# Running sums by head taken from a transposition of the running sums by token

## The reference, cut to what matters

```python
xn = _layernorm(x)
x_branch, z_branch = split(xn @ in_proj_w.T)
x_branch = silu(conv4(x_branch) + conv_b)
proj = x_branch @ x_proj_w.T            # X (1024), dt (16 heads), B (128), C (128)
dt = softplus(dt @ dt_proj_w.T + dt_proj_b)
A_scaled = -exp(A_log) * dt             # one number for each token and head
A_cumsum = cumsum(A_scaled)             # within a chunk
L = exp(A_cumsum[l] - A_cumsum[s])      # for s <= l, for each head
Y_diag = einsum(C, B, L, X * dt)
...                                     # the state of the chunks before, decayed
Y = (Y + X * D) * silu(z_branch)
x + Y @ out_proj_w.T + W3 (sigmoid(W1 xn) * (W2 xn))
```

## Time and profile before

| | |
|---|---|
| time, median of 3 runs | 1618.42 us (1616.63 to 1618.63) |
| the profiled execution, its own time | 1617.01 us |
| its span | 1615.2 us |
| busy: PE, DVE, ACT, POOL | 1559.1, 1203.7, 886.9, 495.6 us |
| mean granted clock of TensorE | 0.989 |
| block 0, from the start to the first sums (L571) | 65.0 us |
| distance of two later blocks, L571 to L571 (484.93 to 678.50) | 193.6 us |

### The profile page before, as it was taken

The page is one execution under the profiler, slowest core; times in us unless marked ns, Lnnn a source line. Parts: engine busy times, 40 slices in busy tenths (PEclk is TensorE's granted clock), DMA queues, the critical chain, the costliest instruction groups (busy, mean ns, idle before and its releaser), DMA issues.

```text
span 1615.2 us, 25318 instructions
## 1 busy us (share of the span) xinstructions
PE 1559.1 (97%) x9086; PEld 744.3 (46%) x9086; DVE 1203.7 (75%) x1876; ACT 886.9 (55%) x1840; POOL 495.6 (31%) x480
## 2 busy tenths in 40 slices
PE   7779899999999999999999999999999999999999
PEld 3334444544444444444444444444444544444444
DVE  7878776699566985689856897568966699576862
ACT  6687435565356644466454663646636565356641
POOL 3116664233033321234221431314303233033210
PEclk9799999999999999999999999999999999999999
DMA  7155430242402432133321333213350242402320
GB/s 266 55 168 175 140 105 14 62 104 74 89 27 68 99 97 56 37 86 85 85 53 47 81 97 92 26 60 89 84 103 14 66 106 71 87 27 73 97 67 26
DMA packets 228605, 131.66 MB, mean 82 GB/s; under 512 B 175200, under 2 KB 176992, under 8 KB 228480
## 3 DMA queue, kind: packets, MB, share of 16 engines
q1 hardware_dynamic: 228480, 130.05, 30.0%
HBM read 100.38 MB, written 29.62 MB: 80 GB/s over the span
## 4 chain that ended last, share of the span: by engine, by line
PE 62%; DVE 18%; issue 7%; ACT 5%; DMA 2%; POOL 2%; SPq 1%; DVEq 0%; POOLq 0%; ACTq 0%
PE bank L723 12%; PE bank L613 11%; PE bank L741 9%; PE bank L507 9%; PE bank L523 6%; PE bank L533 4%; DVE edc L1365 4%; PE bank L696 4%; DVE xst_lo L1336 2%; ACT edc L985 2%; PE bank L645 1%; DVE xin L1407 1%; DVE xdt L1315 1%; ACT mdc L997 1%; DVE xs L1414 1%
## 5 line engine op out<-in xcount | busy, mean ns | idle before, releaser
L613 PE MATMUL bank<-wx_hi,arena 128*128 128x512 f16 x1024 | 319.7, 382 | 0.0
L723 PE MATMUL bank<-xt_hi,q 128*128 128x512 f16 x704 | 267.0, 379 | 4.0 <-issue 4.0
L723 PE MATMUL bank<-xt_lo,q 128*128 128x512 f16 x704 | 267.0, 379 | 0.0
L1688 POOL TENSOR_TENSOR xst<-xdt,dst 128x512 f32<-128x512 f32 x60 | 62.6, 1043 | 490.3 <-DVE xdt L1315 490.3
L613 PE MATMUL bank<-wx_lo,arena 128*128 128x512 f16 x512 | 195.9, 383 | 0.0
L741 PE MATMUL bank<-q,arena 128*128 128x512 fp8e4 x704 | 163.3, 381 | 0.0
L985 ACT ACTIVATE edc<-csl,csv 128x128 f32<-128x128 f32 x512 | 155.8, 389 | 0.8 <-DMA csl<-sums 0.8
L1365 DVE TENSOR_TENSOR edc<-edc,gt 128x512 f32<-128x512 f32 x128 | 125.9, 1022 | 38.7 <-ACT edc L990 38.6
L613 PEld LDWEIGHTS bank<-wx_hi,arena 128*128 128x128 f16 x1024 | 101.1, 99 | 114.7 <-issue 3.7
L1024 ACT CAST arena<-full 128x512 f16<-128x512 f32 x88 | 54.2, 616 | 146.4 <-DVE full L1444 146.4
L1709 POOL TENSOR_TENSOR xin<-xin,xs 128x512 f32<-128x512 f32 x60 | 83.8, 1397 | 153.0 <-DVE xin L1388 153.0
(11 more groups left out here) (217 smaller groups left out, 3419.2 us busy)
## 6 DMA issues: line engine op xcount, KB each, us to landing
csl<-sums SPq DMA_DIRECT2D x128, 256.0 KB, 3.6
y_squares<-xs SPq DMA_DIRECT2D x56, 256.0 KB, 2.0
xin<-y_squares SPq DMA_DIRECT2D x168, 64.0 KB, 2.5
xin<-x SPq DMA_DIRECT2D x32, 256.0 KB, 4.0
res<-x SPq DMA_DIRECT2D x32, 256.0 KB, 3.4
out<-res SPq DMA_DIRECT2D x32, 256.0 KB, 2.0
raw<-w_ffn SPq DMA_DIRECT2D x25, 256.0 KB, 2.9
x_squares<-mdc SPq DMA_DIRECT2D x24, 256.0 KB, 2.0
```

Of the source, the lines that this page charges most:

```text
L613: i = pe.matmul(banks[0][:], act[:, k, c * P:(c + 1) * P], wt[:, k, hf * half:(hf + 1) * half], start=(n == 1), stop=(n == 3 * ki))
L723: i = pe.matmul(up_bank(m, j)[:], q12[:, j, m, k, :], part[:, k, :], start=(n == 1), stop=(n == 2 * kd))
```

## The change

The four products L571 are gone. The sums by head now come from the sums by token: `csv`, 128 tokens by 64 columns (chunk and head), is turned by one transposition on PE (`turn_sums`) to 64 rows by 128 tokens. That instruction stands inside C's product, between its third and fourth part of eight, so behind 9 of 24 matmuls; in block 0, where C is done earlier, it stands behind the transposition of B. `csv` must therefore be there before: DVE's copy waits for the products alone, no longer for ACT. ACT's two exponentials wait for that copy, and ACT's copy to `cst` comes behind them, ahead of the high part of C. `cst` is 64 rows of 128 in place of 16 rows of 512, with the same 64 pieces of 512 bytes in DRAM.

```diff
-        cst = sb("cst", [heads, tb])
+        cst = sb("cst", [chunks * heads, P])
...
-                sp.dma_start(sums.rearrange("c h l -> h c l"),
-                             cst[:].rearrange("h (c l) -> h c l", c=chunks)).then_inc(D["sums_out"], DMA)
+                sp.dma_start(sums.rearrange("c h l -> (c h) l"), cst[:]).then_inc(D["sums_out"], DMA)
...
-            def project(b, bk, col):
+            def project(b, bk, col, between=lambda: None):
                 n = 0
                 for k in range(ki):
+                    if k == 3:
+                        between()
...
-                pe.wait_ge(S["acc"], at(b, "acc", 6))
-                for c in range(chunks):
-                    i = pe.matmul(banks[6][0:heads, c * P:(c + 1) * P], sml["av"][:, c, :], upp[:],
-                                  start=True, stop=True)
-                i.then_inc(S["cst_mm"], 1)
                 pe.matmul(banks[5][:, 0:w], upp[:], v["av"], start=True, stop=True)
                 pe.matmul(banks[5][:, w:2 * w], ones[:], v["av"], start=True, stop=True).then_inc(
                     S["cs_mm"], 1)
+
+            def turn_sums(b):
+                pe.wait_ge(S["acc"], at(b, "acc", 6))
+                pe.wait_ge(S["cs_rest"], at(b, "cs_rest", 0))
+                pe.transpose(banks[6][0:chunks * heads, 0:P], v["csv"], idn[:]).then_inc(S["cst_mm"], 1)
...
-                    project(b, c_bank(b), di + ns).then_inc(S["c_mm"], 1)
+                    project(b, c_bank(b), di + ns, lambda: turn_sums(b)).then_inc(S["c_mm"], 1)
                 turn_b(b)
+                if b == 0:
+                    turn_sums(b)
                 project_x(b, 0, lambda: gram(b))
...
+                act.wait_ge(S["cs_rest"], at(b, "cs_rest", 0))
+                act.activation(v["ecs"], banks[5][:, 0:w], ACT.Exp).then_inc(S["ecs_dec"], 1)
+                act.activation(v["dec"], banks[5][:, w:2 * w], ACT.Exp).then_inc(S["ecs_dec"], 1)
                 act.wait_ge(S["cst_mm"], at(b, "cst_mm", 0))
                 if b:
                     act.wait_ge(D["sums_out"], b * DMA)
-                act.copy(cst[:], banks[6][0:heads, :]).then_inc(S["cst"], 1)
-                act.wait_ge(S["cs_mm"], at(b, "cs_mm", 0))
-                act.activation(v["ecs"], banks[5][:, 0:w], ACT.Exp).then_inc(S["ecs_dec"], 1)
-                act.activation(v["dec"], banks[5][:, w:2 * w], ACT.Exp).then_inc(S["ecs_dec"], 1)
+                act.copy(cst[:], banks[6][0:w, 0:P]).then_inc(S["cst"], 1)
                 act.wait_ge(S["c_mm"], at(b, "c_mm", 0))
...
-                dve.wait_ge(S["ecs_dec"], at(b, "ecs_dec", 1))
+                dve.wait_ge(S["cs_mm"], at(b, "cs_mm", 0))
                 dve.tensor_copy(v["csv"], banks[5][:, 0:w]).then_inc(S["cs_rest"], 1)
                 dve.wait_ge(S["cs_rest"], at(b, "cs_rest", 0))
+                dve.wait_ge(S["ecs_dec"], at(b, "ecs_dec", 1))
```

## The result

The changed kernel takes 1619.72 us (median of 20 runs, 1616.49 to 1624.0), the kernel before 1617.43 beside it (20 runs, 1614.74 to 1620.3). That lies within the 0.2% that the forecast calls no difference, and within its range. But I had forecast 0.2 us less, and twenty runs of each tell the two apart: the sign is wrong, and the sum is 3 us off.

What follows compares the result with a forecast made beforehand. PE's work laid end to end was taken to bound the later blocks, ACT's copy of X to pace block 0. Seven later blocks -2.4 us and block 0 +2.2 gave -0.2 against 1618.4: 1618.2 us, range 1614.2 to 1621.8.

Steps and rivals of the forecast that it cites:

- PE's three terms: Later blocks, PE: C's product 0.92 us earlier, transposition adding 0.13, no standing for `csv`; net gain 0.79 a block.
- The wait of ACT for `csl`: Later blocks: ACT, drawn earlier by PE, waits 0.45 us for `csl` before its decay, a wait not there before.
- the +2.2 for X's copy: Block 0: ACT's copy of X, taken to set the pace, comes 2.2 us later, carried through the block.
- the case I took it from: Block 0: the clock rises as long after X's start as now, so X is done 2.05 us later.
- the case in which ACT's decay sets the copy: Block 0: the clock rises at the same time as now; the decay holds ACT to 80.6, +1.95 us.
- clock stays low: Block 0: PE runs X at 1.2 GHz to its end, costing 5.3 us; 1621.3 us in all; chance 0.05.
- the sum of the later blocks: Blocks 1 to 7: the scan starts 0.34 us earlier, all behind it shifted alike; -2.4 us in seven.
- I take 1.6: Later blocks: the sums' store, now from 64 partitions, lands 1.6 us after issue, 0.3 to either side.
- Slack enough: Later blocks: the sums are back before ACT asks, each block gains 0.79 us; 1615.1 us; chance 0.18.
- Block 0 absorbs its delay: Block 0: its delay vanishes in PE's idle time, leaving -2.4 us, 1616.0 us; chance 0.15.
- `csv` comes too late: Later blocks: `csv` over 1 us late, PE stands inside C; adds to the slower side; chance 0.03.
- The store takes longer: slower: Later blocks: store from 64 partitions, or transposition, takes longer; at 0.6 us more +4.0, 1622.4 us; chance 0.12.

Runs made afterwards that it cites:

- run 8: Kernel before, but storing a tile of zeros, 64 partitions by 128 columns, in place of the sums: 1618.23 us, ratio 1.0009.
- block0_only: Block 0 as in the changed kernel, blocks 1 to 7 as in the kernel before: 1619.92 us, ratio 1.0019.
- part2: Changed kernel with the transposition behind 6 of C's 24 matmuls in place of 9: 1616.70 us, ratio 0.9999.
- part6: Changed kernel with the transposition behind 18 of C's 24 matmuls in place of 9: 1636.64 us, ratio 1.0117.
- c_high_first: Changed kernel, but in block 0 ACT makes C's high part ahead of the exponentials and the copy to `cst`: 1619.70 us, ratio 1.0021.
- run 6: Changed kernel with block 0 as before; in later blocks transposition behind 3 matmuls, `csv` copied ahead of B's low part: 1612.38 us, ratio 0.9981.
- run 2: The same run as `block0_only`: kernel before with only block 0 as in the changed kernel: 1619.92 us, ratio 1.0019.
- runs 1 and 10: Changed kernel with block 0 as before the change; the same kernel timed twice: 1616.85 us, ratio 0.9995, then 1615.90 us, ratio 0.9988.
- run 4: The same run as `part6`: changed kernel with the transposition behind 18 of C's matmuls in place of 9: 1636.64 us, ratio 1.0117.
- runs 7 and 11: Changed kernel, `csv` copied before B's low part, in block 0 between weight splits and transposed before B; later transposition behind 3 matmuls: 1613.54 us; behind nine: 1616.75.

## Why the prediction was wrong

**The mechanisms held.** PE's three terms: C starts 0.47 us behind the first product (0.53 said), the transposition holds PE 0.11 (0.13), no stand for `csv`. ACT's copy takes 0.26 (0.28). The wait of ACT for `csl`, said to be 0.45, came in all seven blocks at 0.29 to 0.97, and the scan waits for `xdt_lo` in all seven. In block 0 the +2.2 for X's copy came as +2.18, though not by the case I took it from, X held back by a late clock. Stretches of the changed kernel, then of the kernel before (PEclk is the third number from the end):

```profile
74.00:76.00 2.00, 2.00 (x5) 0.68 (x6) 2.00 (x4) 0.24 (x2) 0.00 (x0) 0.50 0.18 38
76.00:78.00 2.00, 2.00 (x17) 1.41 (x16) 2.00 (x4) 0.04 (x1) 0.00 (x0) 0.70 0.81 231
```

```profile
74.00:76.00 2.00, 2.00 (x9) 0.80 (x7) 1.90 (x4) 1.79 (x5) 0.00 (x0) 0.69 0.37 121
```

The granted clock leaves its lower level 2.0 us later than before. Those are the 1.97 of this execution's late start: it came back at the same point of the block, and not 1.85 later with X. So the case in which ACT's decay sets the copy held, and X took less time. It is over well before ACT asks for it:

```profile
81.18 0.38 PE L614 MATMUL bank<-wx_hi,arena 128*128 128x512 f16 x1
```

X ends at 81.56 and is copied at 82.82, and the copy's row has no wait: ACT's 4.86 us from the decay's start set it. With my own figure for the decay that case gives +1.95; the decay came 0.23 later than I had it. The rival *clock stays low* falls with the same two rows.

**The step that failed is the sum of the later blocks**, "Behind that the block is as before, shifted by 0.34. Seven blocks: -2.4 us". Against before (16.38 us from the first product to the scan) the seven shifts are -0.21, -0.12, -0.34, -0.45, -0.47, +0.08 and +0.21: **-1.3 us** in all. By time, the two runs with the later blocks alone say -0.8 (-2.3 to +0.6) and -1.9 (-3.4 to -0.3), too wide to show the missing microsecond by themselves; it stands on the rows. The sizes in it, against my own working:

- *The store*, "I take 1.6". It took 1.8 in blocks 1 to 5; run 8 shows that its form does that. 0.2 in five blocks: +1.0 us. It was inside the bounds I gave (0.3), on the bad side.
- *The store in blocks 6 and 7*: 2.31 (1269.72 - 1267.41) and 2.26, so 0.7 over mine: +1.4. Nothing in my sum had it. The decay is there later than it was before the change. These are the stores of the section on the hardware below.
- *Up to the store's issue*: 3.00 us behind the first product (493.89 - 490.89), where my numbers give 3.11: -0.8 in seven.
- *The first load*, from its issue to ACT's start: 3.45 in block 2, 3.09 in block 5 (1079.38 - 1076.29), where I had 3.33 in all. In the seven together -0.7.

They come to +0.9, and the scan's shift is off by +1.1; 0.13 of the rest is block 3, where the second half of `csl` took 3.99 us to land and the relus that need it came later. Rows of SP and ACT in block 6 of the changed kernel:

```profile
1267.41 0.48 SPq L385 DMA_DIRECT2D sums<-cst  x1
1269.72 13.90 SPq L397 DMA_DIRECT2D csl<-sums  x6
```

```profile
1272.87 2.44 ACT L988 ACTIVATE edc<-csl,csv 128x128 f32<-128x128 f32 x8 [0.84 <-DMA csl<-sums]
```

**Block 0's term was taken from one profile.** Its +2.2 is inside the interval of the +3.1 (1.5 to 4.5) timed. But among six profiles with block 0 as before, that one has X's copy latest: 13.68 us behind the first product of the sums, where the others have 12.69 to 13.46, and all six 13.05 on average. The four with block 0 as in the change (`block0_only`, `part2`, `part6` and the changed kernel) have 15.77, so +2.7. From the first products of block 0 to those of block 1 the six have 227.2 us on average (225.8 to 228.2), the four 229.5 (228.6 to 230.0): +2.3. The changed kernel's own profile against that of before has +4.05, one nearly the shortest of its kind, the other the longest; taking that for the term would be reading noise. PE's granted clock fell twice for 6.8 us between 184 and 204 us there, where before has one fall of 3.4 us. The stretch of the second fall, changed kernel, then before:

```profile
190.00:200.00 10.00, 6.83 (x30) 3.03 (x28) 7.45 (x12) 1.12 (x2) 6.68 (x5) 0.67 0.04 6
```

```profile
190.00:200.00 10.00, 6.71 (x34) 3.34 (x35) 6.03 (x12) 2.93 (x6) 5.43 (x4) 1.00 0.47 156
```

All four profiles with the change's block 0 have these two falls of 6.8 us; the six others have falls of 3.4 to 10.2 us in all in this stretch. No experiment shows whether the later X brings them about.

**The sum.** The halves timed alone give +3.1 and, from both runs, -1.4: +1.7, against +2.9 (1.8 to 4.0) for the whole. I had +2.2 and -2.4. The later blocks gave a microsecond less than I had it, and that has its rows, above. Block 0 cost 0.9 more by time and 0.1 to 0.5 more by the profiles, and the whole cost 1.2 more than its halves; both are within what these medians tell, and neither is assigned.

One place where more can go is behind the scan. "Behind that the block is as before" didn't hold in the changed kernel's profile: up to the scan its blocks 1 to 6 gained 1.5 us, but from block 1's first product to block 7's it takes 1161.6 us, as before (1160.2 to 1161.7 in four profiles). PE's wait for `xt_lo` took 1.9 us there against 0.5. By the chain of work it ends with another load from DRAM, `xin<-x_squares`, which has as little slack as `csl`. `c_high_first` has 1162.2 and a wait of 2.2 us; with block 0 as before or repaired, the same later blocks take 1158.6 to 1160.4, with 0 to 0.9 us of it. Whether the late block 0 is the reason isn't shown.

**The rivals.** *Slack enough*: falls, ACT waits in every block. It is what run 6 built: -3.1 us by the ratio, with block 0 out of it. *Block 0 absorbs its delay*: falls by run 2. *`csv` comes too late*: falls, PE takes the transposition in 0.11 us without a wait. *The store takes longer: slower*: its mechanism came, at a third of its price (0.2 of 0.6 us) in five blocks and at 0.7 in two. It is the nearest to what happened, and 0.12 was too little for a step that no row showed. An estimate by the Trainium skill ("DMA: Bandwidth & Descriptors", Anatomy of one DMA) has the two transfers at 4.7 us, by a fit for the software path; the changed kernel's chain has 1.79 + 3.42 = 5.2, so the measured side was the better one, and still short.

## What to carry to other kernels

When work is taken from the engine that bounds a stage, and its result comes instead by a longer way (here a transposition, a store and a load), hold the way's delay against the slack of whoever consumes the result, not against the busy times. Here the loads went out 1.5 us later and ACT came 0.87 earlier, 2.4 together, against 1.8 us of slack: ACT's new wait then took 0.3 to 1.0 us in a block in which 0.87 were saved. Put the new step where its input is just there: with block 0 as before, the same instruction six matmuls earlier and a copy ahead of another one took the gain from 0.8 and 1.9 us (runs 1 and 10) to 3.1 (run 6). Price the first block apart: here it had no cover for what the others hide, and paid more in one block than the other seven gave back.

## What the runs showed of the hardware

- **A store of the same 64 pieces of 512 bytes takes longer from 64 partitions than from 16**: 1.77 to 1.80 us from issue to landing in the seven later blocks of run 8, against 1.58 to 1.60 before; in block 2 the issue itself takes 0.49 us against 0.33.
- **A single packet of kind "instruction" stands beside the long stores.** DMA by queue around the store of block 6, then of block 5, in the changed kernel:

```profile
q1 hardware_dynamic: 80, 0.03, 3.6%
q8 instruction: 1, 0.02, 1.7%
...
sums<-cst SPq DMA_DIRECT2D x1, 32.0 KB, 2.3
```

```profile
q1 hardware_dynamic: 99, 0.07, 5.7%
...
sums<-cst SPq DMA_DIRECT2D x1, 32.0 KB, 1.8
```

  Of the 70 stores from 64 partitions in the later blocks of ten kernels, 10 took 2.01 to 2.80 us from issue to landing, the others 1.77 to 1.83. All 10 are in blocks 6 and 7, and beside each such a packet begins, between 0.02 us before the issue and 0.60 behind it. Of the other 60, four have a packet that begins between 0.5 us before the issue and the landing, but at 0.24 before or 1.5 to 1.6 behind, and took 1.78 to 1.79. No experiment separates them, so this is a coincidence in every case and not a cause shown.
- **PE's clock fell behind waits of 2.6 us in blocks that are otherwise full** (run 4), four times in seven blocks, while in the changed kernel, with waits of up to 1.6 us, it stayed at full level from block 1 on. The waits of the three other blocks (2.4 to 2.7 us) were not followed by a fall. An estimate from the lengths of blocks with and without a fall, 196.0 and 195.35 us, is 0.7 us for a fall, so 2.6 of that run's 16.9 us.
- **Two executions of the same block 0 differ by 2 us and more**: 225.8 to 228.2 us in six profiles, and 228.1 and 224.5 in runs 7 and 11, whose block 0 is the same. The start before it took 64.5 to 67.0 us in the thirteen profiles. One profile beside one profile can't give a term of this size; the times of 11 or 20 runs come within some 1.5 us of it.
